# Two-layer graph network on one core: the opening loads, batch 0's x in halves, the last scalings on ScalarE, and new orders on all engines

## What is computed

```python
u = jnp.einsum('bnh,bmh->bnm', hidden_state, hidden_state) / temper
scores = jax.nn.softmax(u, axis=-1)
delta = scores * adjacency_matrix
att = delta / (jnp.sum(delta, axis=2, keepdims=True) + EPS_RENORM)
...
ctx = jnp.einsum('bnm,bmh->bnh', att_left, h_left) + ... self ... + ... right ...
o = ln_w * ((ctx - mu) / jnp.sqrt(var + EPS_LN)) + ln_b      # then relu
...
d_inv_sqrt = (jnp.sum(adj, axis=-1) + 1e-05) ** (-0.5)
adj_norm = d_inv_sqrt[..., :, None] * adj * d_inv_sqrt[..., None, :]
support = jnp.einsum('bni,io->bno', x, weight)
return jnp.einsum('bnm,bmo->bno', adj_norm, support) + bias
...
x = _layernorm(x + layer0(x, adj)); x = _layernorm(x + layer1(x, adj))
```

## Time and profile before

| | |
|---|---|
| median of 3 runs | 441.21 us (440.77 to 441.22) |
| the profiled execution | 440.96 us |
| its span | 439.4 us |
| PE busy | 429.3 us (98%) |
| DVE busy | 381.1 us (87%) |
| ACT busy | 315.8 us (72%) |
| POOL busy | 302.6 us (69%) |
| share of PE in the chain that ended last | 95% |
| DMA moved | 79.90 MB, mean 182 GB/s |

### The profile page before, as it was taken

How to read it: one execution, slowest core, us unless ns; L and a number is a source line. 1 busy time by engine, 2 the same in 40 slices (tenths; PEclk the granted TensorE clock), 3 DMA queues, 4 the chain that set the end, 5 groups by cost and what they waited for, 6 DMA issues and landing times.

```text
span 439.4 us, 9038 instructions
## 1 busy us (share of the span) xinstructions
PE 429.3 (98%) x2761; PEld 353.6 (80%) x2761; DVE 381.1 (87%) x699; ACT 315.8 (72%) x660; POOL 302.6 (69%) x364
## 2 busy tenths in 40 slices
PE   7999999999999999999999999999999999999994
PEld 5689978779787888869887797977978789896753
DVE  2998999998999889997999989999799989998546
ACT  2689887868777787678876787676867777888420
POOL 2125666668776678758796687866877597797874
PEclk9999999999999999999999999999999999999998
DMA  5935878489665985478944888539866589244802
GB/s 160 357 98 137 265 183 240 155 200 262 141 191 137 265 231 144 146 176 274 226 138 116 213 272 213 161 99 217 285 152 189 135 229 300 60 110 108 191 25 73
DMA packets 68879, 79.90 MB, mean 182 GB/s; under 512 B 7232, under 2 KB 60608, under 8 KB 68832
## 3 DMA queue, kind: packets, MB, share of 16 engines
q1 hardware_dynamic: 68768, 79.26, 66.5%
q0 software_dynamic: 64, 0.07, 0.1%
HBM read 38.40 MB, written 4.19 MB: 97 GB/s over the span
## 4 chain that ended last, share of the span: by engine, by line
PE 95%; DMA 2%; DVE 1%; SPq 1%; issue 0%; ACT 0%; POOLq 0%; POOL 0%
PE ps_y L542 23%; PE ps_c L522 23%; PE ps_d L507 13%; PE ps_c L528 6%; PE ps_u L488 5%; PE ps_u L442 4%; PE ps_u L444 4%; PE ps_u L443 4%; PE ps_m L554 3%; PE ps_m L442 3%; PE ps_m L444 2%; PE ps_m L443 2%; DMA bias_bc<-in_L_gnn_bs_dram 2%; PE ps_u L542 1%; SPq L353 0%
## 5 line engine op out<-in xcount | busy, mean ns | idle before, releaser
L1487 POOL TENSOR_TENSOR dM<-dT,parts 128x384 f32<-128x384 f32 x64 | 72.0, 1126 | 64.1 <-ACT dT L860 52.1
L522 PE MATMUL ps_c<-h_sum,dT 128*128 128x128 f32 x896 | 110.4, 275 | 0.0
L522 PEld LDWEIGHTS ps_c<-h_sum,dT 128*128 128x128 f32 x896 | 106.4, 192 | 2.9 <-issue 2.5
L542 PE MATMUL ps_y<-aT,x1p 128*128 128x512 f32 x224 | 106.3, 593 | 0.0
L847 ACT ACTIVATE d_rows<-ps_u,nmax 128x1024 f32<-128x1024 f32 x62 | 68.8, 1109 | 50.2 <-DVE nmax L1130 50.2
L1130 DVE TENSOR_REDUCE nmax<-ps_u 128x1 f32<-128x1024 f32 x62 | 75.2, 1213 | 17.7 <-PE ps_u L488 15.9
L1137 DVE CUSTOM_DVE_ANT_0 d_rows<-d_rows,a_rows 128x1024 f32<-128x1024 f32 x64 | 84.2, 1323 | 0.3
L860 ACT ACTIVATE dT<-ps_d 128x1024 f32<-128x1024 f32 x64 | 65.3, 1020 | 25.7 <-PE ps_d L507 23.4
L1144 DVE STREAM_TRANSPOSE a_blk<-a_rows 128x1024 f32<-128x1024 f32 x64 | 77.7, 1228 | 0.0
L866 ACT ACTIVATE junk<-a_rows 128x1024 fp8e4<-128x1024 f32 x64 | 67.1, 1049 | 0.3
L507 PEld LDWEIGHTS ps_d<-parts,d_rows 128*128 128x128 f32 x512 | 58.9, 141 | 10.3 <-issue 9.5
(11 more groups left out here) (104 smaller groups left out, 743.7 us busy)
## 6 DMA issues: line engine op xcount, KB each, us to landing
a_rows<-in_adj_dram SPq DMA_DIRECT2D x64, 512.0 KB, 5.0
aT<-a_blk SPq DMA_DIRECT2D x224, 128.0 KB, 3.2
x_rows<-in_x_dram SPq DMA_DIRECT2D x8, 512.0 KB, 3.9
a_rows<-a_blk SPq DMA_DIRECT2D x32, 128.0 KB, 2.4
out_dram<-fin SPq DMA_DIRECT2D x15, 256.0 KB, 2.5
x_turned<-x_blk SPq DMA_DIRECT2D x96, 32.0 KB, 2.2
out_dram<-fin SPq DMA_DIRECT2D x1, 192.0 KB, 2.1
fin<-in_L_gnn_Wl_dram SPq DMA_DIRECT2D x1, 64.0 KB, 3.4
```

Source lines behind the costliest of these rows:

```text
L522: pe.matmul(ps_c[:, c_place(b, i), :], dT[:, i % 2, j, :], h_sum[:, b % 2, j, k * H:(k + 1) * H], start=t == 0, stop=False)
L542: last = pe.matmul(y_bank(b, i0, i1), gathered(b)[:, j, :], turned(b)[:, i0:i1, :, j, :].rearrange("p i q c -> p (i q) c"), start=j == 0, ...
L1487: pool.tensor_tensor(dM[:, i % 2, :, :], dT[:, i % 2, i, :].rearrange("p (a c) -> p a c", a=1).to_broadcast([P, 3, P]), parts[:, :, :], AL ...
```

## The change

- **Opening loads.** x of batch 0 comes as two loads of four blocks, each with a semaphore (`load_x_half`), so the first group of transposes waits for the first half only. The three bias loads are issued by GpSimd, ahead of its constants, and so are the norm constants (ln_w, ln_b, b1), behind them; before, SP issued both. GpSimd makes the identity first of the constants, and TensorE waits for two of them instead of six. The adjacency rows follow the weights on SP at once, in another order. The dummy products read 128 columns of zeros, repeated, and have 512 and 256 columns instead of 512 and 384.
- **Opening work.** Projections of batch 0 alternate between the banks `ps_m` and `ps_y` (`h_bank`), so a projection waits for the addition before the last. The first half of a score row of batch 0 waits for the first half of x alone. Both groups of x transposes stand ahead of the weights' on TensorE, and score rows 0 and 1 ahead of the first projection.
- **Last scalings.** The final scalings of blocks 0 to 6 of the last batch go from VectorE to ScalarE, which also issues the store of blocks 4 to 6. Block 7's scaling, on VectorE, subtracts the mean and multiplies by the power, so it needs no shift from GpSimd. The statistics of blocks 4 to 6 have one variance and one mean step instead of two each.
- **Orders.** All three lists of all five engines are written in another order; the loop is also cut at another place (its first call on TensorE is now `m_read_h(p, 5)`), so steps that stood at the end of one list stand at the start of the next. The number of products, and of the large steps of each engine, is the same.

```diff
         def norm_f_on(eng, b, i0, i1):
-            eng.wait_ge(f_scale, NB * b + i1)
+            eng.wait_ge(f_scale if shifted(b, i1) else f_power, NB * b + i1)
             for i in range(i0, i1):
...
+                else:
+                    last = eng.tensor_scalar(v, v, stats_last[:, 0, 1:2], by, ALU.subtract, ALU.mult)
...
+            def load_x_half(b, half):
+                sp.dma_start(x_rows[:, b, blocks_of(half), :], x_block_rows(x, b, HALF * half, HALF * (half + 1)))\
+                  .then_inc(x_in[b] if half else x0_in, 16)
...
-                load_x(p)
+                load_x_half(p, 0)
+                load_x_half(p, 1)
                 load_weights()
-                load_biases()
                 load_a(p, 0)
-                load_a(p, 3)
                 load_a(p, 1)
                 load_a(p, 2)
+                load_a(p, 7)
+                load_a(p, 3)
+                load_x(b)
...
                 for c in (slice(j0 * P, HALF), slice(max(j0 * P, HALF), N)):
+                    if b == 0 and i < HB:
+                        pe.wait_ge(xt_split, 2 if c.start else 1)
...
+                if b == 0 and j % 2:
+                    pe.wait_ge(xt_split, 2)
+                    wait(pe, h_added, j - 1)
                 s = slice(j * P, (j + 1) * P)
-                split_matmul(ps_m[:, 0:3 * H], xT_hi[:, b % 2, s], xT_lo[:, b % 2, s], wT_hi[:, :], wT_lo[:, :])\
+                split_matmul(h_bank(b, j), xT_hi[:, b % 2, s], xT_lo[:, b % 2, s], wT_hi[:, :], wT_lo[:, :])\
...
             first_products()
-            pe.wait_ge(const_gp, 6)
+            pe.wait_ge(const_gp, 2)
...
+            def store(b, i0, i1):
+                act.wait_ge(f_norm, NB * b + i1)
+                act.dma_start(x_block_rows(out, b, i0 * P, i1 * P), fin[:, i0:i1, :]).then_inc(fin_free[i0 // HB], 16)
...
+                norm_f(b, 0, HB)
+                norm_f(b, HB, NB - 1)
+                store(b, HB, NB - 1)
...
                 add_out(b, NB - 1, NB)
-                norm_f(b, 0, HB)
                 stats_f(b, NB - 1, NB)
-                norm_f(b, HB, NB - 1)
                 norm_f(b, NB - 1, NB)
...
             def constants():
-                pool.memset(parts[:, 0:2, :], 1.0).then_inc(const_gp, 1)
-                pool.memset(parts[:, 2, :], 0.0).then_inc(const_gp, 1)
-                pool.memset(minus_half[:, :], -0.5).then_inc(const_gp, 1)
-                pool.wait_ge(const_gp, 3)
+                for k, v in enumerate((bl, br, bs)):
+                    pool.dma_start(bias_bc[:, k * H:(k + 1) * H], v.partition_broadcast(P)).then_inc(bias_in, 16)
+                pool.memset(ident, 0.0).then_inc(const_gp, 1)
+                pool.wait_ge(const_gp, 1)
```

815 lines of the change are left out of this document (410 added, 405 removed).

## The result

The changed kernel takes 444.75 us (median of six runs, 443.44 to 445.85); the kernel before, timed beside it, 440.9 (440.28 to 441.22, six runs). The ratio is 1.0083, 95% interval 1.0063 to 1.0103: slower by 3.9 us, where 4.2 us less had been forecast. The profiled execution is the fastest of the six, 443.44 with a span of 441.5. So the trace shows 2.1 us of span lost of the 3.9 in the median; what the other executions lose beyond that has no trace.

What follows compares the result with a forecast made beforehand. TensorE, busy 98% of the span, was taken as the bound, so time could be won only at the ends: opening 3.2, loop 0, tail 1.0, together 4.2 us off 440.96, giving 436.8, or 437.0 as median; range 435.8 to 440.8.

Steps and rivals of the forecast that it cites:

- Opening, step 1, the weights: Opening on TensorE: the second x half adds one issue, about 0.47, so the last weight lands at 6.2.
- rival A: Opening: the small loads don't come earlier, weights land up to 2 us later; opening worth 1.2, total 439.0; chance 17%.
- the third turn: TensorE's third turn of masked scores of batch 0, the opening's mark: forecast to start at 19.5 instead of 23.07.
- The forecast's own signs of being wrong: Last weight landing after 7, score rows 0 and 1 at the lower level, or a loop turn over 52.5.
- Opening, steps 2 to 4, the walk: Opening on TensorE and VectorE: first maximum at 8.1, the third turn at 19.5; gain 3.2, bounds 1.3 to 3.8.
- Adjacency row 0 "needed at 11.6": Opening: first adjacency row needed by VectorE's first mask product at 11.6, issued a microsecond earlier than before.
- GpSimd's issues: Opening: three bias loads issued in 2.0 to 3.9 us; identity ready at 3.3 or 5.2, nothing lost up to about 5.
- The loop: Batch loop: the new order costs 0, with 0 to 0.3 us a turn as bounds, covered by slacks.
- Rival B: The loop stalls where lower-half gather steps wait for x1p of the upper half; slower, 443.0; chance 12%.
- The tail: Last 7.6 us: 1.0 us gained of 1.4, ScalarE's store being the later end; bounds 0.5 to 1.4.
- (a, b): Tail on VectorE: statistics directly follow the last addition, 1.0 us less; last scaling without GpSimd's shift, 0.3 less.
- The bounds of the sum: Whole kernel: the opening's and the tail's bounds taken together, 435.8 to 438.4 for the main case, given 60%.

Runs made afterwards that it cites:

- e5: Changed kernel with GpSimd's three bias loads each reading 128 different rows instead of one row 128 times (same size, wrong values): 440.45 us, ratio 0.9979.
- e1: Changed kernel with the three bias loads issued by SyncE again, behind the weights and ahead of the first adjacency row: 442.67 us, ratio 1.0024.
- e3: Changed kernel with three more dummy products of 512 columns on TensorE between the transposes of x and of the weights: 442.18 us, ratio 1.0012.
- e2: Changed kernel with SyncE waiting for the three weights to land before issuing the first adjacency row: 442.78 us, ratio 1.0031.
- e16: Kernel before with e13's loads alone, all orders of the work as they were: 443.00 us, ratio 1.0038.
- e13: Changed kernel with bias rows loaded by ScalarE and spread by TensorE, and SyncE waiting for the weights before the adjacency rows: 439.41 us, ratio 0.9962.
- e7: Changed kernel with the orders of the kernel before on all five engines from the third turn of batch 0 on: 443.99 us, ratio 1.0056.
- e8: Changed kernel with the edits of e6 and e7 at once: 441.30 us, ratio 0.9986.
- e14: Changed kernel with e13's loads and the orders of the kernel before from the third turn of batch 0 on: 439.11 us, ratio 0.9954.
- e4: Kernel before with the changed tail alone, all other orders as before: 440.86 us, ratio 1.0000.
- e9: e6's kernel with the three weight loads issued by ScalarE ahead of its bias rows, beside SyncE's x loads: 444.46 us, ratio 1.0076.
- e12: Kernel before with its opening loads alone changed: weights and bias rows issued by ScalarE, bias spread by TensorE: 447.32 us, ratio 1.0127.
- e6: Changed kernel without bias broadcasts by DMA: ScalarE loads three rows of 512 bytes, TensorE spreads them, ScalarE copies the result: 441.48 us, ratio 1.0014.

## Why the prediction was wrong

- **What bounds the kernel.** Right: TensorE's order is the span, and the middle could only lose.
- **Opening, step 1, the weights.** This step failed. "The last lands at 5.75 + 0.47 = 6.2" took the landing before and added issue time; it was 8.80. It was rival A's mechanism (the broadcasts on GpSimd's queue mix with the weights): with 128 different rows in their place the last weight landed at 6.46 (e5), with the biases behind the weights at 5.71 (e1). But A's price of up to 2 us was too low, in two ways. The delay against the forecast was 2.6, and score rows 0 and 1 ran at the lower clock level, which the sum had at nothing (1.6 us from the last weight to the third turn, against e3). Together they are 4.2 of the 4.3 by which the third turn missed 19.5 (23.79). That a late weight brings the lower level is not a rule here: e2's did not, and e5 and e16 had it with under 0.5 us of idle time. A was given 17% and a gain of 2.2 left. The forecast's own signs of being wrong caught both parts (a last weight after 7, rows 0 and 1 at the lower level). The reason against it, "the weights go in ahead of most of the bias rows", did not fit the order of the issues: two of the three bias issues (1.31 and 2.09) precede the second weight's (2.38), and the third precedes the last weight's. The evidence had been in the earlier trace rows: a bias landing 7.0 us after its issue said that broadcasts are slow; moving them beside the critical loads could only share that slowness.
- **Opening, steps 2 to 4, the walk.** Right within some tenths once the loads are: from the last weight to the third turn 13.42 in e3 and 13.63 in e13 (14.47 less the added product), against 13.3. The start of it was too short and was saved by earlier weights: first maximum 8.19 in e1 against 8.1, but 2.48 behind the weight, not 1.9. Adjacency row 0 "needed at 11.6" was not questioned by the forecast; in e1 it came at 13.85 behind the slow broadcasts.
- **GpSimd's issues.** The three took 1.9 us (1.31 to 3.18) and the identity was ready at 3.9, inside the bounds of 2.0 to 3.9 and at their near end. It cost nothing that shows. By the Trainium skill (DMA: Bandwidth & Descriptors, section on the anatomy of one DMA on the SWDGE path), many descriptors can be emitted before their count shows in the issue; the trace agrees: three loads of 128 rows took 0.55 to 0.78 each, two of 64 rows had taken 1.31 together.
- **The loop.** "Cost of the loop: 0, with 0 to 0.3 a turn as bounds" was mis-sized within its bounds: 0.17 a turn, 0.7 over the four turns measured, and about as much again in the first and last batches: 1.24 in all. Rival B's place (x1p of the upper half) was not it; some handovers of about a tenth of a microsecond are what the starts show. Walks with prices rounded to 0.05 can't see them, and a busy column of 100% can't either. That the order is the cause is shown by e7, e8 and e14, whose turns are 52.3; which handover costs what is read, not tried.
- **The tail.** "1.0 us is left of 1.4" failed at its size: 0.3 in e4, 0.1 in the changed kernel. VectorE's side was right (a, b). In e4 ScalarE's scalings ended at 436.7, which is 436.3 in the times of the kernel before (e4's last products start 0.4 later), not at 435.7, since they waited 0.77 for GpSimd's shift, behind GpSimd's power. This stood in the bounds ("0.5 ... if ScalarE's scalings wait for GpSimd's shift") and should have been the main value: the shift's time was in the order of the work. In the changed kernel 0.2 of the remaining 0.3 went: GpSimd's power starts 1.31 after TensorE's last products, 1.08 in e4, waiting for VectorE, whose variance step at 433.55 took 0.57 (0.17 in e4) while GpSimd added bias rows in its new order (433.38, 0.73 long). This was read from the traces and not tried.

- **The bounds of the sum.** The low end, 435.8, is 440.96 less both upper gains (3.8 and 1.4). The high end, 438.4, doesn't follow from the lower gains: 440.96 less 1.3 and 0.5 is 439.2. The range given in the end went to 440.8 and was missed all the same.

The sum as measured, in span: 0.7 - (-3.2) is 3.9 for the opening, 1.2 for the middle, 0.9 for the tail; and 0.2 ahead of the last products: 6.2. The forecast's span was 435.2 (436.8 less 1.6), the measured one 441.5: 6.3. Outside the span the profiled execution had 1.9 us instead of 1.6.

## What to carry to other kernels

A load that takes long after its issue is a warning, not a constant: find out what makes it slow before moving it, since it will slow what it is moved beside. Loads that the first products wait for did best with few others beside them, by their place in one queue and by a wait behind them (e13); issuing them sooner on another queue while large loads start was the worse choice (e9, e12). But the same loads made the kernel with the old opening order slower (e16), so measure, don't assume. An idle gap of TensorE in the opening can cost more than its length; with a few dummy products in it (e3) the executions agreed within 1.1 us. Shortening one of two chains at the end is worth only what the other allows.

## What the runs showed of the hardware

- Loads of 64 KB that repeat one row of 512 bytes 128 times are slow in company. Of three, the first landed 3.5 to 3.6 us after its issue and the last 5.7 (changed kernel) or 7.0 (before); of six close together three took 8.0 to 10.5 (e1), and from 6 to 10 us the whole traffic was 40 to 62 GB/s. (The three norm constants, issued at 25.1 to 26.1 in the kernel before, took 3.4 to 4.1.) The same bytes from 128 rows left the last weight at 6.46 instead of 8.80 (e5). Three rows of 512 bytes, a product of 0.84 us and a copy of 0.49 on ScalarE do the same work (e13).
- 64 KB on ScalarE's queue beside five loads of 512 KB on SyncE's took 5.5 us (e9), against 2.8 on SyncE's queue behind x and two other weights, with the adjacency rows held back (e13).
- The length of an idle time does not tell TensorE's level in the opening. The passes behind it were at the lower level after 2.84 us (changed kernel), 1.0 us (e8) and 0.49 us (e5), and at the higher one after 2.14 us (e2) and 0.83 us (before). In e16 they were at the lower one until 13.8 us with no idle time above 0.45. With the same loads and opening, e6's profiled execution (439.83) was at the higher level and e8's (443.53) at the lower; the medians of e6's two groups lie 3.7 us apart (439.69 and 443.40).
- The granted clock of a stretch read 0.50 in the changed kernel and e9, and 1.00 in e5, e8 and e16, while in all of them the passes of 512 columns stood 0.43 us apart.
